# Attention heads of a two-layer transformer block: DVE and ACT exchange which of four PSUM copies each makes

## What is computed

```python
scores = jnp.einsum('bhqd,bhkd->bhqk', q, k) / np.sqrt(hd)
scores = scores + _alibi_causal_mask(S, scores.dtype)   # layer 1: a plain causal mask
probs = jax.nn.softmax(scores, axis=-1)
out = jnp.einsum('bhqk,bhkd->bhqd', probs, v)
```

## Time and profile before

| | |
|---|---|
| median of three runs | 2232.56 us |
| the profiled execution | 2237.4 us |
| its span, first to last instruction | 2235.6 us |
| busy, share of the span: PE, DVE, ACT, POOL | 91%, 81%, 71%, 52% |
| layer 0's heads, in the span | about 35 to 312 us |
| layer 1's heads, two runs of 8 | about 491 to 517 us, 556 to 588 us |

### The profile page before, as it was taken

How to read it: one execution, slowest core, us unless ns; L and a number is a source line. 1 busy time by engine, 2 the same in 40 slices (tenths; PEclk the granted TensorE clock), 3 DMA queues, 4 the chain that set the end, 5 groups by cost and what they waited for, 6 DMA issues and landing times.

```text
span 2235.6 us, 82638 instructions
## 1 busy us (share of the span) xinstructions
PE 2033.6 (91%) x34491; PEld 1473.6 (66%) x34491; DVE 1806.9 (81%) x3751; ACT 1578.8 (71%) x3031; POOL 1165.9 (52%) x1413
## 2 busy tenths in 40 slices
PE   6888899987789998999999999999999999999997
PEld 4666564444567776777767777777667777677764
DVE  6778775467778888898888888888889888888884
ACT  4666753345557778877878777777777787877773
POOL 1111110000277666767666767676676676766761
PEclk9999999998889999999999999999999999999999
DMA  4000000000122223322232223222233222332221
GB/s 111 2 2 2 2 1 0 1 1 1 48 75 63 67 60 85 85 69 67 74 85 74 68 60 101 69 71 71 57 91 81 72 70 57 92 80 66 76 57 39
DMA packets 94676, 125.83 MB, mean 56 GB/s; under 512 B 27484, under 2 KB 42466, under 8 KB 94306
## 3 DMA queue, kind: packets, MB, share of 16 engines
q1 hardware_dynamic: 94306, 120.54, 20.7%
HBM read 21.91 MB, written 1.05 MB: 10 GB/s over the span
## 4 chain that ended last, share of the span: by engine, by line
PE 59%; DVE 10%; ACT 5%; issue 4%; POOL 1%; SPq 0%; DMA 0%; POOLq 0%; ACTq 0%; DVEq 0%
PE oo L565 16%; PE pj L565 15%; PE tr L568 13%; PE sc L565 12%; ACT arena L1891 3%; PE tr L565 2%; DVE arena L1699 2%; DVE xn L1292 2%; DVE arena L1701 1%; DVE arena L1720 1%; DVE arena L1722 1%; PE oo L568 1%; ACT xcur L1891 1%; ACT sc L1891 1%; DVE arena L1707 1%
## 5 line engine op out<-in xcount | busy, mean ns | idle before, releaser
L2309 POOL TENSOR_TENSOR arena<-arena 128x1024 f32<-128x1024 f32 x192 | 457.1, 2381 | 349.6 <-DVE arena L1701 349.6
L1891 ACT ACTIVATE arena<-tr 128x512 f32<-128x512 f32 (+2 forms) x874 | 462.2, 571 | 161.3 <-PE tr L568 112.3
L1891 ACT ACTIVATE arena<-pj 128x512 f32<-128x512 f32 x576 | 341.6, 599 | 191.1 <-PE pj L565 154.8
L568 PE MATMUL tr<-ident,arena 128*128 128x128 f32 x2978 | 429.6, 279 | 28.9 <-DMA beta<-in_L_attn_betas 9.9
L568 PEld LDWEIGHTS tr<-ident,arena 128*128 128x128 f32 x2978 | 342.3, 142 | 116.7 <-issue 51.8
L1891 ACT ACTIVATE arena<-arena 128x16 f32<-128x16 f32 (+6 forms) x808 | 355.3, 453 | 57.5 <-DVE arena L1460 26.7
L2327 POOL TENSOR_TENSOR arena<-arena 128x1024 f32<-128x1024 f32 x192 | 366.1, 1907 | 23.2 <-POOL arena L2320 0.9
L1699 DVE TENSOR_TENSOR arena<-pj,rtab 128x512 f32<-128x512 f32 x384 | 259.9, 677 | 30.1 <-ACT arena L1891 28.4
L565 PE MATMUL oo<-slab,arena 64*32 64x64 f32 (+1 forms) x12416 | 231.3, 229 | 42.2 <-issue 27.8
L1701 DVE TENSOR_TENSOR arena<-pj,rtab 128x512 f32<-128x512 f32 x384 | 261.5, 681 | 0.0
L1707 DVE TENSOR_REDUCE arena<-arena 128x8 f32<-128x512 f32 x384 | 255.8, 677 | 0.0
(11 more groups left out here) (288 smaller groups left out, 3816.4 us busy)
## 6 DMA issues: line engine op xcount, KB each, us to landing
slab<-arena SPq DMA_DIRECT2D x576, 128.0 KB, 2.4
slab<-arena SPq DMA_DIRECT2D x336, 64.0 KB, 2.0
wqkv<-in_L_ffn_Wqkv SPq DMA_DIRECT2D x18, 512.0 KB, 4.6
wo<-in_L_ffn_Wo SPq DMA_DIRECT2D x6, 512.0 KB, 4.3
w<-in_L_ffn_W SPq DMA_DIRECT2D x6, 341.0 KB
YT<-in_L_attn_x SPq DMA_DIRECT2D x4, 256.0 KB, 4.1
arena<-in_L_ffn_W SPq DMA_DIRECT2D x1, 1024.0 KB
out_x<-arena SPq DMA_DIRECT2D x4, 256.0 KB, 2.2
```

Of the source, the lines that this page charges most:

```text
L568: return nc.tensor.transpose(o, i, ident[0:i.shape[0], 0:i.shape[0]])
L1891: return nc.scalar.activation(o, i, f, **k)
L2309: p_.tensor_tensor(r_, r_, rb[:, k, :], ALU.add).then_inc(sum_ok, 1)
```

## The change

DVE makes the copies C(0) and C(2) in place of C(1) and C(3), and ACT makes C(1) and C(3) in place of C(0) and C(2). The wait of PE for the copy three blocks back names the other semaphore accordingly. `weigh_ready` waits for both semaphores as before. No instruction is added or taken away on any engine.

```diff
@@ PE, heads
-                                pe.wait_ge((pe_act, pe_dve)[ii % 2], (hb + hh) * 2 + ii // 2 + 1)
+                                pe.wait_ge((pe_dve, pe_act)[ii % 2], (hb + hh) * 2 + ii // 2 + 1)
@@ DVE, heads
-                        if h > h0 and i % 2 == 1:
+                        if h > h0 and i % 2 == 0:
@@ ACT, heads
-                        if h > h0 and i % 2 == 0:
+                        if h > h0 and i % 2 == 1:
```

## The result

The kernel after took 2242.49 us, the median of 14 runs (2235.01 to 2249.73); the kernel before on the same chip took 2232.37 (14 runs, 2227.08 to 2237.76). The ratio is 1.0049, with a 95% interval of [1.0035, 1.0063]: about 11 us slower by the ratio (10.1 by the medians), outside the 0.2% that a measurement of this kernel can tell from nothing. The profiled execution of after took 2241.98 (span 2240.2, mean granted clock 0.981). That of before had lain 5 us above its own median, so the two spans differ by 4.6 us only: the heads of both layers are 11.4 us longer, and all the rest, which the change doesn't touch, happened to be 6.8 shorter. Differences are therefore read stage by stage.

The account below looks back on a forecast made before the run. DVE was taken to set the pace in most heads, PE while weighing, ACT at fill ends and in layer 1's first heads. Terms summed to +8.8 us, 2246.2 for the profiled execution, forecast 2241; range 2229 to 2249.

Parts of the forecast that it names:

- Fill heads, +9.9: Layer 0's fill heads except h % 16 = 13: `low` waits longer for ACT's `high`, 18 x 0.55 us.
- Weighing heads, +3.3: Layer 0's 9 weighings whose preceding head has no fill: PE starts 0.37 us later, waiting for ACT's C(3).
- h % 4 = 2, -3.3: Seven such layer 0 heads where DVE stays the bound: 0.47 us less each from T(1).
- The heads with h % 4 = 3 and no fill: Four layer 0 heads following those with h % 4 = 2: DVE's saving counts, 4 x -0.26 = -1.0 us.
- the -0.27 of the group result: Two groups where the next T(3) waits for PE, and PE for ACT's group result: 2 x -0.27 = -0.5 us.
- The first heads and the last, -0.8: The first heads and the last: 0.8 us less, stated without working.
- Prices of copies: Estimated copy steps: ACT 0.27 us (256-wide) and 0.49 (512-wide); DVE 0.21 (128) and 0.47 (384).
- Layer 1, +1.0 at the first weighing: Layer 1's first heads, ACT-bound: C(3) of head 4 ends later, so PE weighs at 505.07, not 504.04.
- DVE is the bound and nothing else: Rival: -0.26 us in the 64 - 15 heads where PE does not weigh, -12.7 us, 2220; chance 0.11.
- No difference: Rival: only half the fill heads' charge shows, 3.8 us, 2236, not told from no change; chance 0.22.
- PE's lead goes: Rival: block 2's transposes wait for ACT's C(3) of the head before; 9 us more, 2250; chance 0.10.

Follow-up runs that it names:

- fill_delay: The kernel before plus one unused 128x512 ACT copy ahead of `high` in each fill head; 2248.19 us against 2235.20, ratio 1.0061.
- early_new: The change, but ACT's copies C(1) and C(3) no longer wait for T(1) and T(3); 2232.82 us against before's 2235.99, ratio 0.9978.
- fill_old: The change, but with the old hands in layer 0's 21 fill heads; 2234.60 us against before's 2235.99, ratio 0.9988.
- layer0_new: The kernel before with the change in layer 0 only; 2241.84 us against before's 2230.14, ratio 1.0050.
- layer1_new: The kernel before with the change in layer 1 only; 2229.03 us against before's 2228.76, ratio 1.0004.
- early_weigh: The change, but ACT copies before waiting for T in layer 0's h % 4 = 0 heads without a fill; 2243.93 us against before's 2228.76, ratio 1.0072.
- mixed: Against before: ACT copies early everywhere, hands chosen per kind of head (old, the change's, or DVE copying C(1) to C(3) behind T(3)); 2211.94 us, ratio 0.9934.
- early_old: The kernel before, old hands, but ACT's copies C(0) and C(2) no longer wait for T(0) and T(2); 2220.35 us against 2230.14, ratio 0.9952.
- high_pair: The kernel before with only C(2) and C(3) exchanged: DVE makes C(1) and C(2); 2254.11 us against 2235.99, ratio 1.0079.

## Why the prediction was right, and where its terms were off

The forecast was +8.8 us and 2241; the measurement is +10 to +11 and 2242.5. The sign rested on one step, that the chain over T(3), ACT's C(3), E(3) and `high` gets longer although DVE's work gets shorter. In head 39 that chain came out within 0.01 us (4.24 against 4.25), and fill_delay, early_new and fill_old show it as the cause from three sides: adding such a delay alone loses the time, and taking it away in either of two ways brings the total back.

**Fill heads, +9.9: the mechanism right, the size too small.** They lost 13.1. Nine of them lost the 0.55 that was priced; heads 3, 19, 35, 7, 28 and 44 lost 0.2 to 0.7 more, in sum 2.6 (head 31 hardly more, 0.61), and they lost the same in layer0_new, which has the change's hands in layer 0. (Heads 4 and 15 lost 0.4 and 0.2 more, but a stretch of PE at its lower clock lies in each; without one, head 15 lost 0.53 in layer0_new.) The step that failed is "For the others that makes 18 x 0.55", which took ACT as free when a fill head begins. In head 35 it is not: it comes late from C(3) and E(3) of the head before, through the group result and a norm's output; in heads 3, 28 and 44 it is late without a group result, has no pause left, and is itself what `high` waits for. The prediction had ACT's group result 0.34 later, but counted it in two heads without a fill only.

**Weighing heads, +3.3: too large.** In five of the nine places the pair of heads lost 0.58 - 0.27 = 0.31, near the 0.37. But heads 17, 33 and 61 lost nothing. What sets them apart in the trace of before is further work of DVE within the weighing head, 3.9 to 4.3 us busy against 2.7 to 2.9 in the six others. That DVE's lighter copies count there for this reason is not shown, and why they make up for the whole later start stays open. The pair at head 49 lost 1.0, with a stretch at the lower clock in head 48; in layer0_new, without one there, it lost the usual 0.27. The nine pairs came to +1.2.

**h % 4 = 2, -3.3: right in sum (-3.0), mixed inside.** Six heads gained 0.41 of the 0.47; in heads 22, 38 and 54 DVE next takes a product of PE (`xcur`), and now gets there before it is ready; 0.12 is left. Head 22 after, where T(3) starts at 136.64 and would be over at 137.25:

```profile
137.54 0.81 DVE L1426 TENSOR_SCALAR xcur<-oo,bout,modT 128x512 f32<-128x512 f32 x1 [0.22 <-PE oo L565]
```

Before, the same instruction started without a wait, 0.60 after C(3). The heads with h % 4 = 3 and no fill gained 0.27 in four cases, as priced (0.26). In heads 11 and 51 the price was wrong, +0.21 for the -0.27 of the group result: T(3) waits for it longer than was worked out. early_new, where ACT comes earlier, has -0.27 there.

**The first heads and the last, -0.8,** had no working in the prediction; heads 0, 1 and 62 came to -0.9.

**Prices of copies: right.** ACT's 256-wide took 382 ns and a step of 0.28 (estimate 0.27), its 512-wide 597 ns and a step of 0.49 to 0.50 (0.49), DVE's 128 and 384 steps of 0.21 and 0.47 as estimated. The Trainium skill (VectorE: DVE Perf Modes, section on the TRN2 errata) had by its formula an estimate of 357 and 570 ns for the two of ACT; the measured ones are 5 to 7% above, and they decide.

**Layer 1, +1.0 at the first weighing.** Timelines of ACT and PE after, T(0) of head 0 at 500.25:

```profile
513.55 0.60 ACT L1891 ACTIVATE arena<-tr 128x512 f32<-128x512 f32 x1
...
514.20 0.86 PE L565 MATMUL oo<-arena,VhB 128*32 128x128 f32 x24 [0.64 <-ACT arena L1891]
```

The weighing of head 5 starts 13.95 after T(0), against 504.04 - 491.10 = 12.94 before: +1.01. In the total, layer1_new cannot tell it from nothing, and within the first run of heads 0.6 of it is left at the last T(0).

**The rivals.** *DVE is the bound and nothing else* asked for `low` within 3.70 of T(0); it was 4.24. *No difference* asked that half the fill charge be hidden by other waits; none of it was. *PE's lead goes* did not come: the only waits of T(3) for ACT are the five at a group result, 4.1 us, and not 30 at the transposes.

So the sum was right partly by compensation, a term 3 too small beside one 2 too large; all of layer 0's heads come to +9.8 in the two profiles, for which the prediction's terms give +7.6. That the total came within 2 us of the forecast is so in part luck.

## To carry to other kernels

An even split of work by busy time says little about a chain that crosses engines. Follow the chain that someone waits for, and ask of every instruction moved onto its engine whether it stands ahead of that chain's link or behind it: the same four copies, in the same hands, cost 11 us with ACT's wait ahead of them and nothing with it behind them. In a list with a fixed order, put work that is ready ahead of the wait that it does not need, and give an engine that will stand waiting for another the work that the other has in front of the awaited result. Price a moved instruction also for the heads after it: the engine that took it comes late to whatever is next in its list.

## What the runs showed of the hardware that had not been expected

PE stood for 2.4 us at the end of a fill, waiting, and the granted clock then fell to its lower level for about three microseconds inside the weighing that followed. Windows of PE after (us, PE busy and instructions, granted clock, DMA share, GB/s):

```profile
238.00:240.40 2.40, 0.07 (x1) 1.00 0.00 0
240.40:242.00 1.60, 1.56 (x32) 1.00 0.00 0
242.00:243.00 1.00, 1.00 (x25) 0.51 0.00 0
243.00:244.00 1.00, 1.00 (x10) 0.50 0.00 0
244.00:245.00 1.00, 1.00 (x9) 0.50 0.00 0
245.00:246.00 1.00, 1.00 (x17) 0.78 0.00 0
```

0.5 is 1.2 GHz of 2.4. A head that PE bounds takes some 1.5 us longer through it. That is the +1.55 and -1.54 at h % 16 = 13 in the table of heads, where the stretch only fell into another head, and the three odd heads of fill_delay. early_weigh had 13 such stretches in its first 340 us against 5 in before's profile. The mean clock from 34 to 304 us, early_weigh and then mixed:

```profile
34.00:304.00 270.00, 223.00 (x2120) 160.95 (x2121) 190.38 (x762) 189.28 (x394) 47.57 (x70) 0.92 0.02 2
```

```profile
34.00:304.00 270.00, 235.27 (x2405) 172.27 (x2405) 222.29 (x865) 202.89 (x429) 50.55 (x78) 0.98 0.02 2
```

0.92 and 0.98, with before at 0.97 and after at 0.95. The mean over all runs of a kernel goes the same way in several of them: 0.9797 in early_weigh, 0.9788 in fill_delay and 0.9778 in layer0_new, against 0.9857 in mixed and 0.9843 in early_old, with 0.981 to 0.983 for before. It does not in all: layer1_new has 0.9841 and fill_old 0.9847 with hardly a gain in time, and high_pair, the slowest, 0.9808. That totals moved by more than the steps in both directions because a longer pause of PE costs clock as well fits these numbers, but it was not isolated by a run of its own and is not shown. Nor do the pauses tell where a stretch falls: in the profile of after PE stood for 2.3 us or more six times in layer 0's heads (ending at 86.6, 128.2, 164.7, 205.5, 240.4 and 258.9), and the clock fell within 2 us only of those that ended at 128.2, 240.4 and 258.9, while the stretches from 47.5, 98.7 and 177.2 lie next to pauses of 1.0 to 1.7 us. So how much of the 11 us is clock and how much is steps stays open; in the two profiles layer 0's heads account for 9.8, the stretches that moved between h % 16 = 13 heads cancel there, and those in heads 4, 15 and 48 don't.
